# In the last phase of a four-phase graph network, GpSimd's first bias addition for the second stream waits for the first stream's normalised tokens

## The reference, cut to what matters

```
def layer(h, (wl, bl, ws, bs, wr, br, g, beta)):        # two layers, l = 0 and 1
    a      = softmax(h @ h.T / sqrt(384))
    delta  = a * adjacency
    attn   = delta / (sum(delta) + 1e-10)
    hl, hs, hr = h @ wl.T + bl, h @ ws.T + bs, h @ wr.T + br
    ctx    = (attn * upper) @ hl + diag(attn) * hs + (attn * lower) @ hr
    o      = (ctx - mean(ctx)) / sqrt(var(ctx) + 1e-12) * g + beta
    return relu(o)
x = x + layer(layer(relu(layernorm(x))))
```

## Time and profile before

| | us |
|---|---|
| median of 3 runs | 2830.8 (2828.3 to 2832.41) |
| the profiled execution | 2825.79 |
| its span, first to last instruction | 2824.0 |
| TensorE busy | 2738.9 (97%) |
| VectorE busy | 2026.3 (72%) |
| GpSimd busy | 1432.6 (51%) |
| ScalarE busy | 1282.2 (45%) |
| mean granted clock of TensorE | 0.995 |

### The profile page before, as it was taken

One profiled execution on the slowest core, in us unless ns is written; L12 is line 12 of the kernel. 1 busy time (PEld: TensorE's weight loads), 2 busy tenths in 40 slices (PEclk: granted clock), 3 DMA queues, 4 the chain that ended last, 5 costly groups with the idle time before them and its releaser, 6 DMA issues.

```text
span 2824.0 us, 86094 instructions
## 1 busy us (share of the span) xinstructions
PE 2738.9 (97%) x34304; PEld 2534.4 (90%) x34304; DVE 2026.3 (72%) x3996; ACT 1282.2 (45%) x2069; POOL 1432.6 (51%) x2507
## 2 busy tenths in 40 slices
PE   6999999999998999999989999999999999999997
PEld 6999999999988999999989999999888888888886
DVE  4666666766687777777767777778667767676676
ACT  3333333333344444444444444444645545445453
POOL 1222112122224555555535555555677777777777
PEclk9999999999999999999999999999999999999999
DMA  4111121211112111111131111112112111121121
GB/s 154 42 61 61 43 80 41 82 41 61 61 55 84 49 48 48 48 48 48 43 100 49 48 48 48 48 48 67 39 39 75 37 44 67 37 72 39 37 74 34
DMA packets 116487, 158.88 MB, mean 56 GB/s; under 512 B 8000, under 2 KB 112320, under 8 KB 116416
## 3 DMA queue, kind: packets, MB, share of 16 engines
q1 hardware_dynamic: 116416, 157.88, 17.1%
HBM read 107.52 MB, written 50.33 MB: 56 GB/s over the span
## 4 chain that ended last, share of the span: by engine, by line
PE 51%; POOL 26%; issue 13%; DVE 5%; ACT 3%; DMA 2%; POOLq 1%; SPq 0%; DVEq 0%; ACTq 0%
PE ps L227 37%; POOL wide L1315 6%; POOL wide L906 5%; POOL wide L897 4%; PE ps L1133 3%; PE ps L1164 2%; PE ps L759 2%; POOL wide L1300 2%; PE ps L782 2%; POOL wide L1304 2%; PE ps L1150 2%; ACT wide L969 2%; PE ps L699 2%; POOL x_rstd L864 1%; POOL rstd L1334 1%
## 5 line engine op out<-in xcount | busy, mean ns | idle before, releaser
L227 PE MATMUL ps<-w_hi,split 128*128 128x384 f32 x4608 | 1268.2, 343 | 8.7 <-ACT wide L935 5.5
L227 PEld LDWEIGHTS ps<-w_hi,split 128*128 128x128 f32 x4608 | 846.3, 190 | 23.8 <-ACT wide L935 6.1
L227 PE MATMUL ps<-split,w_hi 128*128 128x256 f32 x4608 | 863.5, 283 | 1.6 <-DVE split L616 1.6
L227 PE MATMUL ps<-w_lo,split 128*128 128x384 f32 x2304 | 777.3, 337 | 1.2 <-issue 1.2
L227 PEld LDWEIGHTS ps<-split,w_hi 128*128 128x128 f32 x4608 | 723.5, 189 | 23.9 <-issue 12.7
L227 PE MATMUL ps<-split,w_lo 128*128 128x256 f32 x2304 | 575.2, 280 | 0.0
L227 PEld LDWEIGHTS ps<-w_lo,split 128*128 128x128 f32 x2304 | 436.0, 189 | 0.0
L227 PEld LDWEIGHTS ps<-split,w_lo 128*128 128x128 f32 x2304 | 435.2, 189 | 0.0
L906 POOL TENSOR_TENSOR wide<-wide 128x192 f32<-128x192 f32 x256 | 210.4, 851 | 404.3 <-ACT wide L969 404.3
L1315 POOL TENSOR_TENSOR wide<-wide,row 128x192 f32<-128x192 f32 x512 | 310.0, 641 | 32.2 <-ACT wide L1398 32.2
L493 POOL TENSOR_TENSOR rstd<-mv,pos_half 128x2 f32<-128x2 f32 x64 | 44.2, 699 | 448.2 <-DVE mv L667 448.2
(11 more groups left out here) (129 smaller groups left out, 4572.6 us busy)
## 6 DMA issues: line engine op xcount, KB each, us to landing
x_after<-wide SPq DMA_DIRECT2D x96, 384.0 KB, 2.5
xin<-x_after SPq DMA_DIRECT2D x96, 384.0 KB, 3.3
xin<-in_x SPq DMA_DIRECT2D x32, 384.0 KB, 4.1
wide<-in_x SPq DMA_DIRECT2D x32, 384.0 KB, 3.5
wide<-x_after SPq DMA_DIRECT2D x32, 384.0 KB, 4.2
out<-wide SPq DMA_DIRECT2D x32, 384.0 KB, 2.8
w_raw<-in_w SPq DMA_DIRECT2D x4, 2304.0 KB, 11.5
adjin<-in_adj SPq DMA_DIRECT2D x32, 256.0 KB, 3.6
```

The source lines that it names most:

```text
L227: last = nc.tensor.matmul(out, t if tokens_stay else w, w if tokens_stay else t, start=(k == 0), stop=(k == len(pairs) - 1))
```

## The change: a wait ahead of one GpSimd stage

In GpSimd's stage `w(m)` of the last phase, for stream 1, layer 0, m = 0 alone (the word `w0_0.1`), a second wait is put behind the one on ScalarE's copy: GpSimd waits until VectorE's count for stream 0 has reached the event `n_0` of the same round, the end of `ln_0.0`. It applies in all 16 rounds, the one in the seam between the phases included. Nothing else is altered: no instruction that computes, no order, no DMA.

```diff
--- before.py
+++ after.py
@@ -1309,6 +1309,8 @@
                 def stage(s, i):
                     b = bufs[s]
                     pool.wait_ge(act_done[s], AC[s](f"w{m}_{l}", i))
+                    if (s, l, m) == (1, 0, 0):
+                        pool.wait_ge(dve_done[0], DV[0]("n_0", i))
                     if first(s, i):
                         pool.wait_ge(sems.params_in, params_count)
                     for rows, at in quarters():
```

## The result

| | before | after |
|---|---|---|
| median us | 2828.88 (10 runs, the first three among them) | 2818.71 (10 runs, 2813.2 to 2826.09) |
| ratio | | 0.9958 (0.9947 to 0.9969) |
| once more, beside 16 runs of before on one chip | 2827.83 | 2817.69, ratio 0.9965 (0.9951 to 0.9979) |

The change makes the kernel faster by 10.2 us by the medians and 11.9 by the ratio; in the second comparison it is 10.1 and 9.9. The execution that was profiled is the longest of the ten (2826.09 us, granted clock 0.992), and what makes it long lies ahead of the last phase: it reaches the first transposes of `hT_1.0` in the phase at 2015.52 us, while the profiled execution of the same kernel in e5 reaches them at 2007.49. So its span of 2824.3 us says nothing of the gain; the last phase alone does.

A forecast was written before the change was run, and what follows sets the result against it. TensorE, busy 97% of the span, was taken to bound the kernel. 14 rounds x 0.60 + 0.35 gave 8.8 us gained; subtracted from the median of 2830.8 this gave 2822.0 us, range 2819.5 to 2829.5.

The forecast's parts named there:

- The bound and the place: Last phase: TensorE bounds; its recurring wait is layer 1's transposes for ln_0.0, 15 times, 7.0 us in all.
- The length of ln: VectorE's pair of tensor_scalar in ln_0.0: 0.90 us instead of 1.56 once GpSimd's additions no longer run beside it.
- The term per round: TensorE's transposes in the last phase: 0.60 us gained in each of 14 rounds, bounds 0.48 and 0.69.
- the price of being late now and then: First transpose's load and matmul, 0.02 us apart: the reason for taking 0.60 a round, a little under 0.64.
- the second round's share: TensorE in the phase's second round: 0.24 us of idle time, counted within 0.35 us beside the 14 rounds.
- The base: Whole kernel: the median of 2830.8 us, from which the gain of 8.8 us was subtracted.
- The cost on GpSimd and ScalarE: Additions start 0.9 us later, end at 2421.3 to 2422.7; on_0.1 follows; ScalarE's 2.50 us of idleness hides it.
- The cost on the split: VectorE's split of stream 0 beside additions: cast 0.65 to 0.94, subtraction 1.24 to 1.25; TensorE loses about nothing.
- Rival A: Split's cast and subtraction each wait for a whole addition: gain only 4.5 us, time 2826.3; chance 0.2.
- Rival B: No change, 2830.8 us: another TensorE wait takes over, or additions are not what slows ln_0.0; chance 0.1.
- Rival C: Late GpSimd delays ScalarE's on_0.1, copy and swap, stalling TensorE's w10_1.0: slower, 2834 to 2843 us; chance 0.06.

The follow-up runs named there:

- e5: The changed kernel run again unaltered, beside the kernel before on one chip: 2817.69 us against 2827.83, ratio 0.9965.
- e1: The changed kernel, but its added wait asks for an event long over (rasum_0): 2827.39 us, ratio 1.0000 to the kernel before.
- e3: The kernel before, without the added wait, its eight additions replaced by two of two columns each: 2818.32 us, ratio 0.9964 to the kernel before.
- e6: The changed kernel, with w1_0.1 also waiting for t_lo_1 of stream 0, the split's end: 2822.09 us, ratio 0.9983 to the kernel before.
- e4: The changed kernel, but the wait asks for t_lo_1, so all additions follow the split: 2877.52 us, ratio 1.0174 to the kernel before.
- e2: The changed kernel, with the wait moved behind the first of w0_0.1's four additions: 2825.04 us, ratio 0.9986 to the kernel before.

## Why the prediction was right, and wrong by the range

- *The bound and the place.* Right. TensorE's only recurring wait in the phase was the one for `ln_0.0`, and it is gone.
- *The length of ln.* The pair was to take 0.90; it takes 0.87, the value of the row with nothing beside it. GpSimd's small multiplication does not slow it.
- *The steps that failed* are two terms of the sum, not the mechanism. The forecast was 3.3 us too high: 1.3 from the gain per round, 1.9 from the base.
- *The term per round.* I had 0.64 by the starts of the matmuls and 0.69 with the shorter distance behind them, and took 0.60 "as the price of being late now and then", because load and matmul lay 0.02 apart. With 0.87 the load is never late, and the price is nought: a round is 0.68 shorter. Fourteen rounds of 0.68 and 0.4 to 0.5 for the second are 10.0, and the trace has 10.1 for the phase. The term was 0.08 too small, with the second round's share 1.3 us in all.
- *The base.* This put the time outside the range. I subtracted from 2830.8, the median of three runs; the median of ten is 2828.9, and of 21 and 16 more 2828.3 and 2827.8. Subtracting 10.1 from 2828.9 gives 2818.8, against 2818.71 measured. The lower end of the range had a 10.1 gain in it, but only 1.2 us for the spread between runs; three runs that spread over 4 us leave more open than that, and the profiled execution, 5.0 us below their median, was a sign of it.
- *The cost on GpSimd and ScalarE.* Right, but between the likely and the worst end: the additions took 5.55 and ended 6.50 after the start of `ln_0.0`, which is 2422.3 in the prediction's times (2421.9 likely, 2422.7 at worst); 0.46 of ScalarE's idle time is left.
- *The cost on the split.* The subtraction took 1.24, the cast 0.81, inside the bounds, and no matmul waited.
- *Rival A* (each part waits for a whole addition) did not come: no subtraction is over 1.25. *Rival B* was tested by e1 to e3. *Rival C* has its place, and nearly its threshold: it was to begin when the additions end 7.6 after the start of `ln_0.0` (2423.4 against 2415.81). At 7.42 no matmul waits (e6), at 8.14 one waits 0.17 (e6, second round), at 9.75 it is 2.01 (e4). In e4 it cost 3.8 a round and not the 2.0 expected there, for the clock that falls was not in the sum.

No kernel that I ran is faster than the changed one by more than the spread of the runs; e3 says that at this place there is nothing left.

## What to carry to other kernels

Where the engine that bounds the kernel waits for a short VectorE operation, look at what GpSimd does beside it: one addition of 0.6 us made the operation 0.4 us longer, and holding the additions back cost nothing, for their results had time. Where nobody waits for the VectorE operation, the same slowing costs nothing either. Delay is free only as far as the idle time of the next engines reaches: additions that ended 1.35 us later than before, and even 2.3 us later (e6), were hidden here; 4.6 us later (e4) brought a stall of 2 us and in most rounds a stretch at half the clock behind it. And when a forecast is a difference of a few us, take the base from as many runs as there are, and put its spread into the range.

## What the runs showed of the hardware

- `tensor_scalar` on 128x384 in VectorE, twice: 0.87 us alone, 1.28 with one GpSimd addition beside it, 1.56 with three. With only a GpSimd operation on two columns overlapping its first 0.12 us, it stays at 0.87.
- VectorE's subtraction with two SBUF inputs goes from 0.96 to at most 1.26 beside additions, and the GpSimd addition beside it from 0.60 to 1.32; so the slowing goes both ways. With one addition beside `tensor_scalar` (e2) it does not: the addition keeps its 0.60, and the pair alone gets longer. The Trainium skill, "SBUF — State Buffer", section "Who interferes with whom", says that of a VectorE instruction in a two-port mode and GpSimd the one that issues first has the shared ports and the other "fully blocks". By the recorded starts e2 does not bear this order out: the addition starts 0.08 after the first `tensor_scalar`, and it is VectorE that is slowed. No run shows whether `tensor_scalar` is in such a mode here. That the two engines meet at these ports is a statement of the Trainium skill; the runs show only that they slow each other.
- A TensorE stall of 2.0 us or more inside the dense stream came with about 3.4 us at 1.2 GHz in 13 of the 16 rounds of e4. The stalls of the other three (2.00 to 2.14) and the one of 1.95 in e6 did not, nor did the stalls of 0.2 to 0.5 of the kernel before, in any round of the phase.
